# Reordering the mixes, the division and GpSimd's queue in a chunked RWKV block with a routed expert layer

## The reference

```
x  = x + layernorm(attn(layernorm(x)))
   attn: xn = ln1(x); xx = token_shift(xn)
         xk, xv, xr = xn*mix + xx*(1-mix)        (three mixes: key, value, receptance)
         k, v, r = xk Wk', xv Wv', xr Wr'
         y  = (e1*aa + e2*v) / (e1*bb + e2)      (aa, bb, pp: a recurrence over tokens)
         x  = x + (sigmoid(r) * y) Wo'
         x  = x + sigmoid(xr2 Wr_ffn') * (relu(xk2 Wk_ffn')^2 Wv_ffn')
x  = x + layernorm(shared(z) + expert[argmax(z Wg)](z)),   z = layernorm(x)
   shared, expert: (gelu(z w1) * (z w2)) w3, with 8 experts
```

## Time and profile before

| | |
|---|---|
| runs | 1026.13, 1027.78, 1030.36 us; median 1027.78 |
| profiled execution | 1025.36 us, span 1023.5 us |
| busy share of the span | PE 91%, PE weight load 82%, DVE 73%, ACT 57%, POOL 56% |
| the chunk stage | 0 to about 687 us |
| the slot stage | from about 687 us to the end |

### The profile page before, as it was taken

The page is one execution under the profiler, slowest core; times in us unless marked ns, Lnnn a source line. Parts: engine busy times, 40 slices in busy tenths (PEclk is TensorE's granted clock), DMA queues, the critical chain, the costliest instruction groups (busy, mean ns, idle before and its releaser), DMA issues.

```text
span 1023.5 us, 28016 instructions
## 1 busy us (share of the span) xinstructions
PE 931.3 (91%) x9734; PEld 838.2 (82%) x9734; DVE 743.4 (73%) x1653; ACT 587.2 (57%) x1014; POOL 577.4 (56%) x800
## 2 busy tenths in 40 slices
PE   3387999999999999999999999779999999999994
PEld 2266888888888888888888888668999999999994
DVE  5989999999999999999999894523444444444442
ACT  4477768768768768768768756323333333333331
POOL 5445757755756756756757632443554555554553
PEclk9687999999999999999999999989999999999997
DMA  7113151251251251251252248466876788486510
GB/s 236 62 53 110 45 207 52 94 207 51 96 208 49 95 205 45 99 205 46 98 205 93 84 156 283 164 222 213 273 259 228 232 294 270 144 275 196 176 55 22
DMA packets 87338, 156.36 MB, mean 153 GB/s; under 512 B 5549, under 2 KB 68142, under 8 KB 82160
## 3 DMA queue, kind: packets, MB, share of 16 engines
q1 hardware_dynamic: 35760, 72.74, 20.8%
q10 hardware_dynamic: 46960, 65.89, 19.8%
q0 software_dynamic: 4560, 16.98, 4.3%
HBM read 178.35 MB, written 50.51 MB: 224 GB/s over the span
## 4 chain that ended last, share of the span: by engine, by line
PE 59%; DVE 25%; issue 8%; DMA 2%; POOL 2%; ACT 2%; SPq 1%; ACTq 1%; DVEq 0%; POOLq 0%
PE up L342 12%; PE up L344 11%; PE up L343 11%; DVE mixed L1008 6%; PE yp L342 6%; PE yp L344 6%; PE yp L343 6%; DVE stats L989 2%; DVE arena L983 2%; PE tp L351 2%; DVE er L1080 1%; DVE gu L1203 1%; PE yp L549 1%; PE yp L546 1%; DVE x L1102 1%
## 5 line engine op out<-in xcount | busy, mean ns | idle before, releaser
L342 PE MATMUL up<-mix_s,arena 128*128 128x128 f16 x1248 | 211.1, 219 | 1.6 <-DMA arena<-w_split 1.6
L343 PE MATMUL up<-mix_s,arena 128*128 128x128 f16 x1248 | 211.1, 219 | 0.0
L344 PE MATMUL up<-mix_s,arena 128*128 128x128 f16 x1248 | 211.1, 219 | 0.0
L342 PE MATMUL up<-xf_s,arena 128*128 128x256 f16 x512 | 140.3, 274 | 2.8 <-issue 1.7
L343 PE MATMUL up<-xf_s,arena 128*128 128x256 f16 x512 | 140.3, 274 | 0.0
L344 PE MATMUL up<-xf_s,arena 128*128 128x256 f16 x512 | 140.3, 274 | 0.0
L1654 POOL TENSOR_TENSOR kf_s<-ex,kf_s 128x512 f16<-128x512 f32 x78 | 90.1, 1156 | 85.2 <-ACT kf_s L942 85.1
L1425 DVE SCALAR_TENSOR_TENSOR ex<-up,ex 128x512 f32<-128x512 f32 x78 | 54.0, 692 | 101.9 <-ACT ex L936 101.4
L342 PEld LDWEIGHTS up<-mix_s,arena 128*128 128x128 f16 x1248 | 122.1, 98 | 2.0 <-DMA arena<-w_split 1.8
L343 PEld LDWEIGHTS up<-mix_s,arena 128*128 128x128 f16 x1248 | 122.1, 98 | 0.4
L344 PEld LDWEIGHTS up<-mix_s,arena 128*128 128x128 f16 x1248 | 122.1, 98 | 0.0
(11 more groups left out here) (228 smaller groups left out, 2902.2 us busy)
## 6 DMA issues: line engine op xcount, KB each, us to landing
arena<-w_split ACTq DMA_DIRECT2D x117, 1024.0 KB
arena<-in_W SPq DMA_DIRECT2D x24, 1024.0 KB, 6.3
w_split<-arena SPq DMA_DIRECT2D x24, 1024.0 KB, 8.9
rows<-routed_rows ACTq DMA_DIRECT2D x39, 261.0 KB, 2.9
routed_rows<-x_in SPq DMA_DIRECT2D x8, 650.0 KB, 6.4
normed<-routed_rows ACTq DMA_DIRECT2D x39, 128.0 KB, 2.6
x_in<-in_x SPq DMA_DIRECT2D x16, 256.0 KB, 2.8
x_res<-in_x SPq DMA_DIRECT2D x16, 256.0 KB, 2.7
```

Source lines behind the costliest of these rows:

```text
L342: pe.matmul(out, stat(0), mov(0), start=first, stop=False)
L343: pe.matmul(out, stat(0), mov(1), start=False, stop=False)
L344: return pe.matmul(out, stat(1), mov(0), start=False, stop=last)
```

## The change

Four things move. On DVE the halo goes ahead of `gate`, `den_r` and `num`; the key's mix goes ahead of `divide`; the value's and the receptance's mix and `carry` go directly behind `rw`, ahead of `x3_gate` and `x3_sum`. `mix0` has two more waits, for `den_r` (m = 0) and for `num` (m = 1), both of DVE itself. On ACT `mix_hi(0)` goes ahead of `sh_hi(1)`, and `mix_hi(1)` and `mix_hi(2)` ahead of `early_hi`. On POOL the scatter goes from ahead of `sh_lo(0)` to behind `sh_lo(1)`, `sh_lo(1)` goes ahead of `mix_lo(1)`, and `mix_lo(2)` ahead of the inverse square roots. No instruction is added or removed.

```diff
@@ ACT
                 sh_hi(0)
+                mix_hi(0)
                 sh_hi(1)
                 if at_step(i, NC + 1):
                     first_slot()
                 late_hi()
-                mix_hi(0)
+                mix_hi(1)
+                mix_hi(2)
                 early_hi()
-                mix_hi(1)
                 own(2)
                 gelu(2)
-                mix_hi(2)
@@ DVE
             def mix0(c, b, m):
                 x = xnT[b]
+                if m == 0:
+                    wait(dve, S("denominator"), 4 * c - 1)
+                if m == 1:
+                    wait(dve, S("num"), c)
                 wait(dve, S("delta"), c + 1)
@@
                     den_now(c0)
+                if on(i + 1):
+                    halo(xnT, i + 1, 1 - p, "halo", "xnT")
                 own(0)
                 if on(c2) and not at_step(i, NC + 1):
                     gate(c2)
@@
                     den_r(c0)
                     num(c0)
                 if on(i + 1):
-                    halo(xnT, i + 1, 1 - p, "halo", "xnT")
+                    mix0(i + 1, 1 - p, 0)
                 if on(c0):
                     divide(c0)
                 late_lo(late_now(i, p, h))
-                if on(i + 1):
-                    mix0(i + 1, 1 - p, 0)
                 if on(c0):
                     rw(c0)
                 if on(i + 1):
                     mix0(i + 1, 1 - p, 1)
+                    mix0(i + 1, 1 - p, 2)
+                    carry(i + 1)
                 if on(c1):
                     x3_gate(c1)
-                if on(i + 1):
-                    carry(i + 1)
-                if on(c1):
                     x3_sum(c1)
-                if on(i + 1):
-                    mix0(i + 1, 1 - p, 2)
@@ POOL
                 delta_of()
-                scatter(c3, 1 - p)
                 scatter_expert_input()
                 sh_lo(0)
                 mix_lo(0)
+                sh_lo(1)
+                scatter(c3, 1 - p)
                 mix_lo(1)
-                sh_lo(1)
+                mix_lo(2)
                 inverse2()
                 offset2()
                 inverse1()
-                mix_lo(2)
                 sh_lo(2)
```

## The result

| | before | after |
|---|---|---|
| median of 6 runs each (us) | 1029.99 | 1035.71 |
| lowest to highest (us) | 1026.13 to 1030.36 | 1034.19 to 1039.9 |
| profiled execution, its span (us) | 1025.36, 1023.5 | 1039.9, 1038.2 |
| ratio to before | 1 | 1.0077 [1.0053, 1.0101] |

The changed kernel is slower by 0.8%, or some 8 us. The ratio is to 1027.78 us, the median of the three runs given with the kernel before; by the two medians of this table it is 5.7 us, 0.6%. 1010.3 was predicted and 1025 was the upper end. The forecast is wrong in size and in sign.

A forecast was written before the change was run, and what follows sets the result against it. DVE sets the pace, PE right behind. PE's 22.6 us of stalls, less 2.1 left over and 3 for the scatter, plus 1.5 at the start, less 1.5 at the end, gave 17.5 us saved: 1010.3 us, range 1004 to 1025.

The forecast's parts named there:

- `x3_sum`, again with two SBUF inputs, stands until 303.7 and ends at 304.3.: Odd step, DVE: the sum waits for POOL's mix_lo(1), begun about 302.5; 1.1 us charged in the even step.
- delays nothing: POOL: mix_lo(2) ahead of the inverses is early for its reader, and DVE's moments end later; no cost.
- 4.3 us per step of DVE are lost to POOL.: Three pairs of mixes in step 7: 6.6 instead of 2.35 us, as two-SBUF-input instructions stand until POOL's is done.
- it stands 0.6 us: Odd step: rw behind the reciprocal waits for POOL's third low half and ends near 300.5; 0.8 us charged in even steps.
- DVE idles 1.9 us: Even step: the moved halo waits for ACT's xnT, with gate, den_r and num queued behind; bounds 0 to 1.9 us.
- I put 0.5 us on each of the six odd steps: Later scatter may land late for x1_sum, shared(3) and projection(2): 3 us in all, ends 0 and 2.4 us a step.
- The slower rival, a late store: The store of rows lands too late, holding x1_sum, shared(3) and projection(2): 9 us lost at 8.5 us landing, 1037; chance 0.07.
- 1.5 us was foreseen, in bounds of 0 to 5: Step 16: the later scatter makes x1_sum late on the path to the slots; 1.5 us lost.
- 1.5 us saved, between -1 and 4.: Steps 0 to 2: the second pair's regained time against the halo's wait for xnT in step 1, together 1.5 us saved.
- Past that PE is the bound: Whole kernel: DVE savings count at most what PE stands still, 22.6 us; beyond that PE limits.
- both kinds of step near 36.7 us apart: Sign of being right: odd and even steps both take about 36.7 us.
- the first (POOL meets other work): Rival: second and third pairs stay blocked, only the key's mix saves 1.38 us; 5 us gained, 1023; chance 0.14.

The follow-up runs named there:

- x3_first: Changed kernel with x3_gate and x3_sum directly behind rw, ahead of the value's and the receptance's mix; 1015.33 us, ratio 0.987.
- mixlo2_late: Changed kernel with mix_lo(2) back behind the inverse square roots on POOL, nothing else; 1025.41 us, ratio 0.9973.
- halo_mid: Changed kernel with the halo moved behind own(0) and gate, ahead of den_r; 1037.84 us, ratio 1.011.
- own_first: Changed kernel with own(0) on DVE ahead of the halo; 1032.44 us, ratio 1.005.
- three: Changed kernel with the edits of x3_first, own_first and scatter_end together; 1007.04 us, ratio 0.9802.
- dve_only: Kernel before with only DVE's new order and its two added waits, ACT and POOL as before; 1018.13 us, ratio 0.9905.
- scatter_end: Changed kernel with the scatter back ahead of sh_lo(0) in steps 15 and 16 alone; 1034.53 us, ratio 1.0063.
- filler: Changed kernel with a DVE memset of about 0.6 us, read by nobody, between x3_gate and x3_sum; 1035.55 us, ratio 1.0086.

## Why the prediction was wrong, point by point

**"`x3_sum`, again with two SBUF inputs, stands until 303.7 and ends at 304.3."** This step failed. It took the work that POOL does behind the scatter to be one `mix_lo`. But the change also puts `mix_lo(2)` right behind it, and by then DVE has done both mixes, so both are ready; from step 3 to 14 POOL runs them in 2.27 us without letting DVE in, where the sum would take 0.69. Priced: 3.01 - 0.69 = 2.3 us in each of these steps, instead of 1.1. The prediction had both facts, the order of POOL's list and the stretched instruction, and said of `mix_lo(2)` that it "delays nothing" because it looked only at who waits for POOL, and not at which DVE instruction stands beside it. DVE's path through a step is then longer than PE's, so that PE waits 1.5 to 1.75 us in each step. x3_first takes this term away and wins 20 us; mixlo2_late takes half of it away and wins 10. That is shown.

**"4.3 us per step of DVE are lost to POOL."** Right, nearly: the mixes give back 4.0. But x3_sum's 2.5 and, in both kinds of step, 0.3 and 0.5 of small things take most of it, and in the even step the halo's 1.9 takes more than is left. The odd step wins 0.8 instead of 2.5 us and the even one loses 1.4 instead of winning 0.5. One of the small things was not seen: the halo ahead of `gate` lets POOL's `delta` start beside it, and `gate`'s 128x2 CAST then has a median of 561 ns (170 before, and 169 in halo_mid, where `gate` comes first). These terms are why mixlo2_late, with the one `mix_lo` that was priced, still doesn't reach 36.7 us a step.

**"it stands 0.6 us" (`rw`).** It took 0.72 us in step 7 and 0.83 in step 6, and stood hardly at all: POOL's three halves ended at 306.05, just behind the reciprocal. A small term, too dear by about 0.5.

**"DVE idles 1.9 us", even step.** Right in size (1.86). It stays in x3_first (15.1 us in 8 waits, as here), where PE is full all the same: once `x3_sum` no longer stands, DVE has room for it.

**The scatter: "I put 0.5 us on each of the six odd steps".** Too dear. Landing took 3.0/3.5/4.6 us (least, median, most; 200 to 350 us) against 3.8/5.5/6.8 before, and `x1_sum` waited for nothing in the middle. The slower rival, a late store, is therefore not what made this kernel slower. It did come in step 16: a wait of 3.37 us for the landing, on the path to the slots. There 1.5 us was foreseen, in bounds of 0 to 5; the end lost 4.8 in all, of which how much is the scatter's is not shown. The scatter's two instructions were counted at 0.97 us and cost more: 1.32 and 1.21 us in step 7 beside four mixes, against 1.06 and 0.97 before, and 3.04 us for the first in step 16 beside an instruction over 128x2048. The Trainium skill's rule (SBUF — State Buffer, "SBUF: two separate sides"), that VectorE can keep GpSimd from writing descriptors, was weighed at nothing. The longer instructions go its way, but no run separates the writing of descriptors from the rest of them.

**Start: "1.5 us saved, between -1 and 4."** It lost 5.0, outside the bounds, and 1.9 to 5.8 in the other kernels with this order at the start. The wait in step 1 had been seen, not that it comes again in step 2 (1.60 us), nor that `rw` behind it makes PE stand 2.48 us there, behind which the granted clock falls to 0.83. With that wait taken away step 3 begins at 115.2 (own_first), 116.6 (halo_mid) and 117.1 us (three), against 117.2 before: 0 to 2 us saved, so the 1.5 that was foreseen is neither shown nor excluded.

**The sum.** "Past that PE is the bound" and "both kinds of step near 36.7 us apart" hold in x3_first and three: 36.8 and 37.0. With the three edits the time is 1007.0, ratio 0.9802; the forecast was 1010.3 of 1027.8, 0.983. So the accounting of what there was to win in the middle is right, and what failed is the claim that this order wins it. That 1007.0 lies near 1010.3 is in part luck, since it is a different kernel. Of the rivals, the first (POOL meets other work) named the kind of mechanism but had it on the mixes, which were freed; it priced a gain of 5 us and it was a loss of 8. None had the instruction that was really hit.

**Still open.** Why two `mix_lo` keep the sum out. The pair alone doesn't do it, nor do its tiles, since in steps 1 and 2 the sum gets in between the same two. Nor does it decide whether the second is ready when the first starts: in step 7 of halo_mid ACT's half ended 0.6 us behind the start of the first, the sum came then, and it stood 2.22 us, for both. What the steps where it is kept out have in common is that the pair follows the scatter's last instruction at once; where DVE gets in (steps 1 and 2, the kernel before, dve_only) POOL had been waiting for ACT ahead of the first of the two. No run has the pair with the scatter elsewhere, so this is a guess. Open too: what the scatter costs the end. The granted clock in a stretch 40 to 50 us behind the start of step 15 is 0.85, 0.87 and 0.90 in the changed kernel, scatter_end and own_first, and 1.00 in the kernel before, x3_first and three, which may be part of what differs there.

## What to carry to other kernels

When work of GpSimd is moved out of the way of one VectorE instruction, look for the next VectorE instruction with two SBUF inputs, and price it with the whole run of GpSimd instructions that are ready then, not with one; then look at the trace, for here the same pair cost 2.3 us in twelve steps and 0.3 in two. Two halves of a change that don't lose alone (-0.95%, -0.3%) can lose together (+0.8%): time them apart and together. A wait of TensorE can cost its clock besides its own length: look at the granted clock behind each wait that a change adds.

## What the runs showed that was not expected

- A VectorE instruction of 0.69 us stood behind two GpSimd instructions in a row: 3.01 us, and 2.45 when it was issued 0.6 us later. The Trainium skill says that a VectorE instruction with two SBUF inputs and a GpSimd instruction that reads SBUF exclude each other, and that the second to issue waits until the first has finished (SBUF — State Buffer, "Summary: rules for kernel authors"). By that it would have waited for one at most, and would have had 1.9 us, as in mixlo2_late. Steps 1 and 2 agree (0.95 us); steps 3 to 14 show a wait for two, also where the sum came first by the records (309.04 against 309.22).
- A CAST of 128x2 numbers, 170 ns by itself, has a median of 561 ns beside a GpSimd instruction of 1.04 us.
- Idle time of 2.48 us in step 2 goes with a granted clock of 0.83 from 110 to 120 us, in five kernels. 2.23 us at the same place in filler does not (1.00), nor do the shorter waits of later steps: it was 1.00 from 196 to 300 us, where PE stood 1.5 to 1.75 us in each step.
